# AdaLN block with four Mamba-2 layers and a mixture of experts: work of the mixer's steps moved between ScalarE and GpSimd, reordered, and four steps per loop body

## The chip, the cores and the metric

The kernel runs on one core of a Trainium2 chip. The metric is the device time of one launch in microseconds. Three runs of the kernel before took 1159.37, 1164.06 and 1163.69 us, median 1163.69 us.

## The reference

The input x has 8 batches of 512 tokens of width 128. With `sa, ca, ga, sb, cb, gb` six modulation vectors per batch:

```python
h = layernorm(x) * (1 + ca) + sa
for l in range(4):                                  # the mixer: four Mamba-2 layers
    n = rmsnorm(h) * block_norm_w[l]
    z, xBC, dt = split(n @ W_in[l])                 # 256, 512, 8 columns
    xBC = silu(causal_conv4(xBC))                   # four taps along the tokens
    xs, B, C = split(xBC)                           # 256, 128, 128
    dt = softplus(dt + dt_bias); dA = exp(-exp(A_log) * dt)
    hs = hs * dA + (dt * xs) B^T ; y = hs C         # a scan over 512 tokens, 8 heads of 32
    y = rmsnorm((y + D * xs) * silu(z)) * gate_norm_w
    h = h + y @ W_out[l]
x = x + ga * rmsnorm(h) * final_norm_w
x = x + gb * moe(layernorm(x) * (1 + cb) + sb)      # shared expert + top 2 of 8 experts
```

## The kernel before, in words

Tokens lie along the free dimension: a tile [128, 512] is one batch, its 128 partitions the model's width. `h` and `xT` hold all eight batches in SBUF. The scan over tokens is computed by chunks: each batch is cut into four chunks of 128 tokens. Within a chunk the result is a masked product of matrices; between chunks a state S of [128, 256] is carried (the recurrence: three states, S1 to S3).

The mixer has 32 steps, one per layer and batch; step k is layer k // 8, batch k % 8. Each engine runs its own list of instructions in order, and engines wait for one another by counting semaphores. The body of step k works on three batches at once: part A projects and convolves batch k, part B does the chunk products and the recurrence of batch j = k-1, part C the gated norm and output projection of batch i2 = k-2, and N prepares the norm of batch k+1. Steps 0 to 2 and 31 to 33 are written out; steps 3 to 30 are loops whose body holds two steps (`pairs_of_steps`, L227), 14 passes. SP and POOL have these 28 steps in three loops (`steps_with_weights`, L246): in steps 3 to 18 they also convert the experts' weights, 256 KB a step, for later (called weight steps here; the others are plain steps). After the mixer come the routing and the shared expert for each batch ("front") and 23 tiles of routed experts.

What a step holds, by engine, with the names used below:

- SP (L299): loads RW (weight steps), WO_raw after `wos_a` says that the one before was scaled, five of the six projection weights WA[t] after PE is done with each, then the small rows PC and P4, then WA[5].
- PE (L474): `dt` product (L487), `decays(0)` (L542, L548), G = B C^T (L573), `turn` of x and B (L527), `decays(1)`, `project(2)` (L494; a projection waits for the taps of the tile that used its bank: project(2) for tap(0,3), project(3) for tap(1,3)), `turn(3)`, `square_mean` (L503, L504; waits for ACT's sqy), `project(3)`, `project_out` (L510, L511), `decays(2)`, `within(0)` (L562; waits for DVE's scale_out, whose bank it overwrites), `project(4)`, `decays(3)`, `within(1)`, the mean of sqh (L619), `project(5)`, transposes (L632 to L634), `within(2)`, the states' products (L640, L641, L644), `within(3)`, two projections of the next step (L667), and `yi` (L658), which needs the states.
- ACT (L946): exponentials E0 to E7 (`decay_exp`, L951; En+2 waits for Mn, two buffers), softplus parts, `xtok` (L971), squares `sqy` (L1000), tap 0 of tiles 2, 3 and 1 (L963, L942), lnY and rY (L1018, L1020), `norm_square` (L850: copies WDT, the dt weights; L853: sqh = h squared), row_exp (L957), zraw (L1044), the scaling of WO (L1052, two of 128x128), `norm_log` and `norm_root` (L857, L862), and six SiLUs with a table load.
- DVE (L1341): conv taps of four tiles (tap(0,0) is L1350, the others L1354; tap(t, s) adds shift s of tile t and waits for the tap before it on that tile), causal (L1361), M0 to M7 (`apply_decay`, L1370), the scan of dA (L1379), `spend` (L1383), scale_out (L1389), `hn` (L1475), the recurrence (L1447, then twice `stmp` L1451 and S L1457), `yt` (L1465) and `ti` (L1470).
- POOL (L1619): dt_ (L1622), dtx and xw (L1630, L1635), the three-part split of cum (L1641 to L1648), wdec (L1650), weight conversion in weight steps (L1665, L1667), the update of h (L1671), own_rows (L1656), then for t = 0, 1 `yt` += `ti` (L1679) and y2 = yt * silu(z) (L1683), which wait for DVE's `ti`.

The order of taps and its neighbours on DVE (L1394):

```python
tap(0, 0); tap(0, 1); tap(0, 2); tap(1, 1); tap(0, 3); tap(1, 2)
causal_products(); apply_decay(0)
apply_decay(1)
tap(1, 3); running_sum()
```

Of the kernel before, what the change touches and what calls it, by code (L numbers as in the profile page):

```python
# [60 lines left out]
def build(nc, x, w_in, w_out, par, cst, c_t, wmod, par2, w1, w2, out):  # L61
    ctx = ExitStack()
    with ctx:
# [137 lines left out]
        wdt_a, hup, sqh_a, ms_mm, rb_a, hn_v = sem("wdt_a"), sem("hup"), sem("sqh_a"), sem("ms_mm"), sem("rb_a"), sem("hn_v")  # L201
# [5 lines left out]
        fin_v, fin_p, wos_a = sem("fin_v"), sem("fin_p"), sem("wos_a")  # L207
# [19 lines left out]
        def pairs_of_steps(eng, body, first, last, **kw):  # L227

            with eng.Fori(first // 2, last // 2) as i:
                for odd in (1, 0):  # L230
                    k = eng.snap(2 * i + (2 - odd))
                    body(k, odd, A=True, B=True, C=True, N=True, **kw)

        def steps(eng, body):


            body(0, 0, A=True, B=False, C=False, N=True)
            body(1, 1, A=True, B=True, C=False, N=True)
            body(2, 0, A=True, B=True, C=True, N=True)
            pairs_of_steps(eng, body, 3, STEPS - 1)  # L240
            body(STEPS - 1, 1, A=True, B=True, C=True, N=False)
            body(STEPS, 0, A=False, B=True, C=True, N=False)
            body(STEPS + 1, 1, A=False, B=False, C=True, N=False)

        def steps_with_weights(eng, body):
# [5 lines left out]
            pairs_of_steps(eng, body, 3, 3 + NE, W="up")  # L251
            pairs_of_steps(eng, body, 3 + NE, 3 + 2 * NE, W="down")
            pairs_of_steps(eng, body, 3 + 2 * NE, STEPS - 1)
# [23 lines left out]
        def _(sp):  # L277
# [26 lines left out]
            def body(k, odd, A, B, C, N, W=None):  # L304
# [6 lines left out]
                if B:  # L311
                    j = k - 1
                    at_j = sp.snap(j // NB * (2 * DM * P))

                    wait(sp, wos_a, 2 * j)
                    sp.dma_start(WO_raw[:, :], rows(w_out, at_j, 2 * DM)).then_inc(s_wo, 16)
# [89 lines left out]
        def _(pe):  # L406
# [30 lines left out]
            pe.wait_ge(sqh_a, 1)  # L437
# [37 lines left out]
            def body(k, odd, A, B, C, N):  # L475
# [5 lines left out]
                if A:  # L481

                    wait(pe, hn_v, k + 1)
                    wait(pe, wdt_a, k + 1)
# [21 lines left out]
                def project_out():  # L506
                    wait(pe, wos_a, 2 * (i2 + 1))
# [86 lines left out]
                if C and not B:  # L594
                    square_mean_of_h(1)
                if A:
                    project(3)
                if C:
                    project_out()
# [16 lines left out]
                if N:  # L616
                    wait(pe, sqh_a, k + 2)
# [199 lines left out]
        def _(act):  # L817
# [30 lines left out]
            def norm_square(n):  # L848
                wait(act, dt_mm, n)
                f(WDT[:, :], PAR[:, bass.ds(n // NB * NPAR + C_WDT, 32)], ACT.Copy).then_inc(wdt_a, 1)  # L850
                wait(act, hup, n + 1)
                wait(act, ms_mm, n)
                f(sqh[:, :], h[:, bass.ds(n % NB * L, L)], ACT.Square).then_inc(sqh_a, 1)  # L853

# [12 lines left out]
            norm_square(0)  # L867
# [77 lines left out]
            def body(k, odd, A, B, C, N):  # L945
# [83 lines left out]
                if N:  # L1029
                    norm_square(k + 1)  # L1030
                elif A:
# [13 lines left out]
                if B:  # L1045
                    row_exp(1)

                    wait(act, s_wo, 16 * (j + 1))
                    wait(act, out_mm, j)
                    gw = act.snap(j // NB * NPAR + C_GW)  # L1050
                    for t in range(2):
                        f(WO[:, t * DM:(t + 1) * DM], WO_raw[:, t * DM:(t + 1) * DM], ACT.Copy,  # L1052
                          scale=PAR[:, bass.ds(gw + t, 1)]).then_inc(wos_a, 1)
# [133 lines left out]
        def _(dve):  # L1187
# [149 lines left out]
            def body(k, odd, A, B, C, N):  # L1337
# [56 lines left out]
                if A:  # L1394
                    tap(0, 0)
                    tap(0, 1)
                    tap(0, 2)
                    tap(1, 1)
                    tap(0, 3)
                    tap(1, 2)  # L1400
                if B:
                    causal_products()
# [203 lines left out]
        def _(pool):  # L1606
# [9 lines left out]

            def body(k, odd, A, B, C, N, W=None):
# [54 lines left out]
                if A:  # L1672
                    own_rows(0)
                    own_rows(1)
                if B:

                    for t in range(2):
# [6 lines left out]

            steps_with_weights(pool, body)
# [121 lines left out]
```

## Time and profile before

| | |
|---|---|
| median of three runs | 1163.69 us |
| the profiled execution | 1162.99 us |
| its span, first to last instruction | 1161.0 us |
| mixer, steps 3 to 30 | about 99 to 751 us |
| busy, share of the span | PE 86%, DVE 84%, ACT 76%, POOL 58% |
| mean granted clock of TensorE | 0.952 |

The profile lists instructions by engine: PE is TensorE's matmul, PEld its weight load, DVE VectorE, ACT ScalarE, POOL GpSimd, SP the queue that issues DMAs. L1383 is line 1383 of the kernel. "Busy" leaves out waits, register and branch instructions. "Idle before" is the time that an engine stood before an instruction, and the name behind the arrow is what ended it; "issue" means that the profile shows nothing that it waited for. The chain that ended last follows the work back from the last instruction to what released each.

### The profile page before, as it was taken

To read this page: it belongs to the slowest core of one execution; us is meant where nothing else is said; L and a number is where in the kernel's file an instruction comes from. 1 tells how busy PE (TensorE), PEld (TensorE's weight loads), DVE (VectorE), ACT (ScalarE), POOL (GpSimd) and SP (SyncE) were. 2 spreads that over 40 slices of the span, in tenths; PEclk is the share of its full clock that TensorE was granted. 3 is DMA by queue.
4 is the path that set the end of the run, shared out by engine and by line. 5 is a ranking of instruction groups with operands and counts; after the bars stand their busy time and mean duration, and the time that the engine had idled before them with its cause. 6 is when DMAs were issued, how large, how long until landed. Compare 5 with 4: busy or idle time off the path is not lost.

```text
span 1161.0 us, 25184 instructions
## 1 busy us (share of the span) xinstructions
PE 993.7 (86%) x6136; PEld 559.7 (48%) x6136; DVE 977.1 (84%) x1801; ACT 884.2 (76%) x1724; POOL 676.3 (58%) x853
## 2 busy tenths in 40 slices
PE   5799999999899999999999999985788767999980
PEld 4244544445444444454445444542444445777760
DVE  6779999999999999999999998974778775888865
ACT  5688999999899999999999999984556534655640
POOL 0267577766776677656655765672244551666661
PEclk9789999999999999999999999998888888999995
DMA  5111242224222432210001000100000115676638
GB/s 141 34 34 33 89 156 86 88 87 153 91 86 87 142 102 86 78 32 22 22 23 31 22 22 23 27 7 1 19 28 28 37 33 180 223 232 226 223 116 217
DMA packets 85584, 97.84 MB, mean 84 GB/s; under 512 B 20698, under 2 KB 65888, under 8 KB 85536
## 3 DMA queue, kind: packets, MB, share of 16 engines
q1 hardware_dynamic: 80544, 88.83, 24.2%
q0 software_dynamic: 4992, 8.48, 2.2%
q8 instruction: 18, 0.29, 0.1%
q14 instruction: 30, 0.25, 0.1%
HBM read 59.67 MB, written 37.83 MB: 84 GB/s over the span
## 4 chain that ended last, share of the span: by engine, by line
PE 35%; DVE 26%; issue 18%; ACT 6%; POOL 3%; DVEq 2%; DMA 1%; ACTq 0%; SPq 0%; POOLq 0%
DVE cv L1354 9%; PE bank L494 4%; PE bank L562 4%; PE bank L681 2%; PE bank L667 2%; DVE M L1370 2%; PE bank L683 2%; PE bank L682 2%; DVE cv L1350 2%; PE bank L619 2%; PE bank L693 2%; PE bank L695 2%; PE bank L692 2%; PE bank L658 2%; PE bank L640 2%
## 5 line engine op out<-in xcount | busy, mean ns | idle before, releaser
L1354 DVE SCALAR_TENSOR_TENSOR cv<-bank,PAR,cv 128x511 f32<-128x511 f32 (+2 forms) x384 | 274.1, 742 | 15.7 <-ACT cv L963 2.8
L1370 DVE SCALAR_TENSOR_TENSOR M<-E,bank 128x512 f32<-128x512 f32 x256 | 168.3, 678 | 20.7 <-ACT E L951 11.4
L1679 POOL TENSOR_TENSOR yt<-yt,ti 128x384 f32<-128x384 f32 x64 | 64.0, 1000 | 203.6 <-DVE ti L1470 203.6
L494 PE MATMUL bank<-hn,WA 128*128 128x512 f32 x256 | 144.9, 649 | 41.0 <-DVE cv L1354 40.6
L951 ACT ACTIVATE E<-bank 128x512 f32<-128x512 f32 x256 | 149.0, 595 | 31.9 <-DVE M L1370 30.1
L1710 POOL DMA_INDIRECT RS<-y,XR x92 | 98.8, 1074 | 78.7 <-DVE y L1567 55.4
L1703 POOL DMA_INDIRECT XS<-stage,IDX x64 | 65.9, 1029 | 79.2 <-DVE run L1329 62.1
L1101 ACT ACTIVATE hr<-bank,W1B 128x512 f32<-128x512 f32 x92 | 63.4, 689 | 56.7 <-PE bank L683 49.8
L562 PE MATMUL bank<-M,dtx 128*32 128x128 f32 x2048 | 82.9, 279 | 15.6 <-DVE o_sb L1389 15.1
L494 PEld LDWEIGHTS bank<-hn,WA 128*128 128x128 f32 x256 | 40.6, 194 | 111.9 <-issue 74.0
L1497 DVE TENSOR_TENSOR hL<-hr,hH 128x512 fp32r<-128x512 f32 x124 | 87.1, 702 | 4.3
L1683 POOL TENSOR_TENSOR y<-yt,zs 128x512 f32<-128x512 f32 x64 | 81.6, 1274 | 9.8 <-POOL yt L1679 7.0
L1656 POOL TENSOR_TENSOR own<-p,selb 128x512 bf16<-128x512 bf16 x64 | 72.7, 1157 | 15.5 <-PE bank L548 15.5
L1630 POOL TENSOR_TENSOR dtx<-xtok,DTW 128x256 f32<-128x256 f32 x128 | 80.6, 630 | 1.0 <-ACT xtok L971 1.0
L562 PEld LDWEIGHTS bank<-M,dtx 128*32 128x32 f32 x2048 | 49.2, 109 | 59.5 <-issue 53.2
L1495 DVE CAST hH<-hr 128x512 fp32r<-128x512 f32 x124 | 54.3, 438 | 25.6 <-ACT hr L1101 12.1
L1082 ACT ACTIVATE xbc<-cv 128x512 f32<-128x512 f32 x128 | 72.9, 619 | 0.0
L667 PE MATMUL bank<-hn,WA 128*128 128x512 f32 x128 | 65.2, 632 | 1.4 <-ACT zs L1086 0.8
L542 PE MATMUL bank<-nselb,PC 32*128 32x512 bf16 x256 | 61.3, 388 | 0.3 <-ACT E L951 0.2
L1635 POOL TENSOR_TENSOR xw<-xtok,DTW 128x256 f32<-128x256 f32 x96 | 60.9, 634 | 0.0
L971 ACT ACTIVATE xtok<-bank 128x384 f32<-128x384 f32 x128 | 56.2, 508 | 2.5 <-PE bank L527 2.4
L658 PEld LDWEIGHTS bank<-xbc,S 128*128 128x128 f32 x384 | 47.6, 191 | 17.8 <-DVE S L1457 13.6
(245 smaller groups left out, 2633.8 us busy)
## 6 DMA issues: line engine op xcount, KB each, us to landing
XS<-PADT SPq DMA_DIRECT2D x32, 520.0 KB, 4.3
WA<-w_in SPq DMA_DIRECT2D x192, 64.0 KB, 1.8
W1B<-WD SPq DMA_DIRECT2D x23, 514.0 KB
W2B<-WD SPq DMA_DIRECT2D x23, 512.5 KB
WD<-WS SPq DMA_DIRECT2D x16, 512.0 KB, 2.7
XR<-XS SPq DMA_DIRECT2D x23, 260.0 KB
RW<-w_in SPq DMA_DIRECT2D x18, 256.0 KB, 4.4
WO_raw<-w_out SPq DMA_DIRECT2D x32, 128.0 KB, 3.6
```

The costliest lines, as they stand in the source:

```text
L494: mm(bank[t % 2][:, :], WA[t][:, :], hn[:, :], start=True, stop=True).then_inc(pj_mm, 1)
L562: ins = mm(bank[6 + hh // 4][q:q + 32, c * CH:(c + 1) * CH], dtx[c][:, hh * HD:(hh + 1) * HD], M[2 * (hh // 4) + c % 2][:, (hh % 4) * CH:( ...
L667: mm(bank[t][:, :], WA[t][:, :], hn[:, :], start=True, stop=True).then_inc(pj_mm, 1)
L951: f(E[i % 2][:, :], bank[2 + i % 2][:, :], ACT.Exp).then_inc(e_a, 1)
L1082: f(conv_rows(t, odd), cv[t][:, :], ACT.Silu).then_inc(silu_a, 1)
L1354: stt(out=cv[t][:, s:L], in0=src[:, 0:L - s], scalar=PAR[:, bass.ds(cw + 3 - s, 1)], in1=cv[t][:, s:L], op0=ALU.mult, op1=ALU.add).then_in ...
L1370: stt(out=M[i % 4][:, :].rearrange("p (n t) -> p n t", n=4), in0=E[i % 2][:, :].rearrange("p (n t) -> p n t", n=4), scalar=1.0, in1=bank[5 ...
L1497: tt(hL[t][:, :], hr[t][:, :], hH[t][:, :].bitcast(F32), ALU.subtract).then_inc(hl_v, 1)
L1630: tt(dtx[c][:, :].rearrange("p (h d) -> p h d", h=NH), xv, DTW[:, 32 * c:32 * c + NH].unsqueeze(2).to_broadcast([P, NH, HD]), ALU.mult).th ...
L1656: tt(own[:, g * 512:(g + 1) * 512].rearrange("p (h t) -> p h t", h=4), p2[:, :].unsqueeze(1).to_broadcast([P, 4, CH]), selb[:, g * 512:(g ...
L1683: tt(y2[t][:, :], yt[t][:, :], zs[:, bass.ds((j % 2) * 2 * L + t * L, L)], ALU.mult).then_inc(fin_p, 1)
L1710: nc.gpsimd.indirect_dma_start(RS[:, :], bass.IndirectOffsetOnAxis(ap=XR[i % XD][:, (c + 1) * ROW - 1:(c + 1) * ROW].bitcast(I32), axis=0) ...
```

## The change

The mixer's steps are changed in five places. On DVE the three shifts of tile 0 follow one another, and tap(1, 2) comes behind the causal product. On PE `project_out` comes ahead of `project(3)`. The square of h for the norm is made by POOL, for the batch after the next, and in most steps waits until DVE has made the second `stmp` of the recurrence (`s_v`, 5j+4); ACT makes only the first one. POOL also copies WDT and scales WO, behind own_rows. The loops have four steps per body: 7 passes on PE, ACT and DVE; 2, 2 and 3 on SP and POOL. In `steps` and `steps_with_weights` every call of `pairs_of_steps` becomes one of `fours_of_steps`; the semaphores are renamed with their engine.

```diff
-        def pairs_of_steps(eng, body, first, last, **kw):
-            with eng.Fori(first // 2, last // 2) as i:
-                for odd in (1, 0):
-                    k = eng.snap(2 * i + (2 - odd))
-                    body(k, odd, A=True, B=True, C=True, N=True, **kw)
+        def fours_of_steps(eng, body, first, last, **kw):
+            with eng.Fori(first // 4, last // 4) as i:
+                for n in range(4):
+                    k = eng.snap(4 * i + (3 + n))
+                    body(k, (3 + n) % 2, A=True, B=True, C=True, N=True, **kw)
...
@@ sync: body, if B @@
-                    wait(sp, wos_a, 2 * j)
+                    wait(sp, wos_p, 2 * j)
                     sp.dma_start(WO_raw[:, :], rows(w_out, at_j, 2 * DM)).then_inc(s_wo, 16)
...
@@ tensor: body @@
                 if C and not B:
                     square_mean_of_h(1)
-                if A:
-                    project(3)
                 if C:
                     project_out()
+                if A:
+                    project(3)
...
@@ scalar @@
-            def norm_square(n):
-                wait(act, dt_mm, n)
-                f(WDT[:, :], PAR[:, bass.ds(n // NB * NPAR + C_WDT, 32)], ACT.Copy).then_inc(wdt_a, 1)
-                wait(act, hup, n + 1)
-                wait(act, ms_mm, n)
-                f(sqh[:, :], h[:, bass.ds(n % NB * L, L)], ACT.Square).then_inc(sqh_a, 1)
...
-            norm_square(0)
+            f(WDT[:, :], PAR[:, C_WDT:C_WDT + 32], ACT.Copy).then_inc(wdt_done, 1)
+            act.wait_ge(hup, 1)
+            f(sqh[:, :], h[:, 0:L], ACT.Square).then_inc(sqh_done, 1)
...
-                if N:
-                    norm_square(k + 1)
-                elif A:
+                if A and not N:
                     square_h(0)
...
-                    wait(act, s_wo, 16 * (j + 1))
-                    wait(act, out_mm, j)
-                    gw = act.snap(j // NB * NPAR + C_GW)
-                    for t in range(2):
-                        f(WO[:, t * DM:(t + 1) * DM], WO_raw[:, t * DM:(t + 1) * DM], ACT.Copy,
-                          scale=PAR[:, bass.ds(gw + t, 1)]).then_inc(wos_a, 1)
                     decay_exp(6)
...
@@ vector: body @@
                     tap(0, 2)
+                    tap(0, 3)
                     tap(1, 1)
-                    tap(0, 3)
+                if B:
+                    causal_products()
+                if A:
                     tap(1, 2)
                 if B:
-                    causal_products()
                     apply_decay(0)
...
@@ gpsimd @@
+            def square_h(n):
+                hb = h[:, bass.ds(n % NB * L, L)]
+                wait(pool, hup, n + 1)
+                wait(pool, ms_mm, n)
+                tt(sqh[:, :], hb, hb, ALU.mult).then_inc(sqh_done, 1)
+
+            def step_weights(n):
+                wait(pool, dt_mm, n)
+                tt(WDT[:, :], PAR[:, bass.ds(pool.snap(n // NB * NPAR + C_WDT), 32)], ones_row[:, 0:32], ALU.mult).then_inc(wdt_done, 1)
+
+            def output_weights(n):
+                gw = pool.snap(n // NB * NPAR + C_GW)
+                wait(pool, s_wo, 16 * (n + 1))
+                wait(pool, out_mm, n)
+                for t in range(2):
+                    tt(WO[:, t * DM:(t + 1) * DM], WO_raw[:, t * DM:(t + 1) * DM], PAR[:, bass.ds(gw + t, 1)].to_broadcast([P, DM]),
+                       ALU.mult).then_inc(wos_p, 1)
...
                     own_rows(0)
                     own_rows(1)
-                if B:
+                if N:
+                    step_weights(k + 1)
+                if B:
+                    output_weights(j)
+                if N and not B:
+                    square_h(k + 2)
+                if B:
+                    if N:
+                        wait(pool, s_v, 5 * j + 4)
+                        square_h(k + 2)
                     for t in range(2):
                         wait(pool, fin_v, 4 * j + 3 + t)
...
+            pool.wait_ge(const_v, 3)
+            square_h(1)
             steps_with_weights(pool, body)
```

## Rows read from the trace of the kernel before

**Rows 1.** Busy us (instructions) of each engine, granted clock, DMA share, GB/s, by stretch
```profile
286.00:477.00 191.00, 176.07 (x1259) 91.34 (x1258) 176.33 (x286) 175.22 (x361) 137.34 (x179) 1.00 0.32 108
477.00:751.00 274.00, 254.29 (x1806) 130.19 (x1804) 250.78 (x416) 252.38 (x523) 172.59 (x238) 1.00 0.09 25
```

**Rows 2.** The chain that ended last, 543 to 569 us: start, us, what
```profile
555.38 0.65 PE bank L562 x16
...
567.42 0.82 DVE cv L1350
```

**Rows 3.** Timeline of DVE, plain steps: start, us, what, [idle before <-releaser]
```profile
560.55 0.69 DVE L1370 SCALAR_TENSOR_TENSOR M<-E,bank 128x512 f32<-128x512 f32 x1 [0.52 <-ACT E L951]
...
563.58 0.42 DVE L1451 TENSOR_TENSOR stmp<-S,dec 128x256 f32<-128x256 f32 x1
...
577.13 0.74 DVE L1354 SCALAR_TENSOR_TENSOR cv<-bank,PAR,cv 128x510 f32<-128x510 f32 x1
577.96 0.69 DVE L1389 TENSOR_TENSOR o_sb<-bank,rY 128x512 f32<-128x512 f32 x1
...
590.36 0.80 DVE L1350 TENSOR_SCALAR cv<-bank,PAR 128x512 f32<-128x512 f32 x1
```

**Rows 4.** Timeline of ACT, one plain step
```profile
550.19 0.60 ACT L951 ACTIVATE E<-bank 128x512 f32<-128x512 f32 x1 [0.65 <-DVE M L1370]
...
553.76 0.21 ACT L850 ACTIVATE WDT<-PAR 128x32 f32 x1
...
554.40 0.76 ACT L963 ACTIVATE cv<-bank,PAR 128x512 f32<-128x512 f32 x1
...
557.17 0.60 ACT L1044 ACTIVATE zraw<-bank 128x512 f32<-128x512 f32 x1 [0.66 <-PE bank L494]
```

**Rows 5.** Timeline of PE, the same step
```profile
548.00 1.12 PE L494 MATMUL bank<-hn,WA 128*128 128x512 f32 x2 [0.61 <-DVE cv L1354]
```

**Rows 6.** Timeline of POOL, the same step
```profile
557.87 2.27 POOL L1656 TENSOR_TENSOR own<-p,selb 128x512 bf16<-128x512 bf16 x2 [1.12 <-PE bank L548]
566.43 0.99 POOL L1679 TENSOR_TENSOR yt<-yt,ti 128x384 f32<-128x384 f32 x1 [6.29 <-DVE ti L1470]
```

**Rows 7.** What line L1350, tap(0,0) on DVE, sat idle for: us, times
```profile
  issue: 5.3, 13
```

**Rows 8.** Timeline of DVE, two weight steps
```profile
188.04 0.75 DVE L1475 SCALAR_TENSOR_TENSOR hn<-h,PAR,rB 128x512 f32<-128x512 f32 x1 [0.26 <-issue]
...
207.38 0.97 DVE L1383 TENSOR_SCALAR spend<-CST,p 128x32 bf16<-128x32 f32 x1
```

**Rows 9.** Timeline of POOL, the same two weight steps
```profile
185.56 2.28 POOL L1656 TENSOR_TENSOR own<-p,selb 128x512 bf16<-128x512 bf16 x2
...
207.03 1.28 POOL L1671 TENSOR_TENSOR h<-h,o_sb 128x512 f32 x1
```

**Rows 10.** Line L1383: duration min/median/max in ns, first and last start
```profile
L1383 DVE TENSOR_SCALAR spend<-CST,p x32: 230/494/1144, 41.4 to 764.9; 128x32 bf16<-128x32 f32 x32
```

**Rows 11.** Line L1379, the scan, likewise
```profile
L1379 DVE TENSOR_TENSOR_SCAN cum<-ones_row,dA x32: 417/703/878, 37.0 to 759.1; 128x128 f32<-128x128 f32 x32
```

**Rows 12.** Groups of ACT, 60 to 830 us: count, busy us, mean ns
```profile
L1052 ACT ACTIVATE WO<-WO_raw,PAR 128x128 f32<-128x128 f32 x64 | 22.1, 400 | 0.0
```

**Rows 13.** Groups of POOL, likewise
```profile
L1650 POOL TENSOR_TENSOR wdec<-dt_,ecs 128x128 f32<-128x128 f32 x31 | 14.1, 455 | 0.0
```

**Rows 14.** Timeline of DVE at the start
```profile
26.20 2.23 DVE L1228 TENSOR_SCALAR sqy<-xin,mv,rstd 128x128 f32 x8 [0.30 <-issue]
```

**Rows 15.** Part 3 of the page: packets, MB, share, of the instruction queues
```profile
q8 instruction: 18, 0.29, 0.1%
q14 instruction: 30, 0.25, 0.1%
```

**Rows 16.** Part 6 of the page: DMA issues, KB each, us to landing
```profile
WA<-w_in SPq DMA_DIRECT2D x192, 64.0 KB, 1.8
...
RW<-w_in SPq DMA_DIRECT2D x18, 256.0 KB, 4.4
```

More of the change, by code:

```diff
@@ L200, in build @@
         s_wo, p4_in = sem("wo_in"), sem("p4_in")
-        wdt_a, hup, sqh_a, ms_mm, rb_a, hn_v = sem("wdt_a"), sem("hup"), sem("sqh_a"), sem("ms_mm"), sem("rb_a"), sem("hn_v")
+        wdt_done, hup, sqh_done, ms_mm, rb_a, hn_v = sem("wdt_done"), sem("hup"), sem("sqh_done"), sem("ms_mm"), sem("rb_a"), sem("hn_v")
         dt_mm, pj_mm, silu_a, dtc_v, dta_a, tr_mm = sem("dt_mm"), sem("pj_mm"), sem("silu_a"), sem("dtc_v"), sem("dta_a"), sem("tr_mm")
@@ L206, in build @@
         px_p, st_mm, s_v, e2_mm, e2_a, yi_mm = sem("px_p"), sem("st_mm"), sem("s_v"), sem("e2_mm"), sem("e2_a"), sem("yi_mm")
-        fin_v, fin_p, wos_a = sem("fin_v"), sem("fin_p"), sem("wos_a")
+        fin_v, fin_p, wos_p = sem("fin_v"), sem("fin_p"), sem("wos_p")
         sq_a, ss_mm, ry_a, out_mm, o_v = sem("sq_a"), sem("ss_mm"), sem("ry_a"), sem("out_mm"), sem("o_v")
@@ L239, in steps @@
             body(2, 0, A=True, B=True, C=True, N=True)
-            pairs_of_steps(eng, body, 3, STEPS - 1)
+            fours_of_steps(eng, body, 3, STEPS - 1)
             body(STEPS - 1, 1, A=True, B=True, C=True, N=False)
@@ L250, in steps_with_weights @@
             body(2, 0, A=True, B=True, C=True, N=True, W="shared")
-            pairs_of_steps(eng, body, 3, 3 + NE, W="up")
-            pairs_of_steps(eng, body, 3 + NE, 3 + 2 * NE, W="down")
-            pairs_of_steps(eng, body, 3 + 2 * NE, STEPS - 1)
+            fours_of_steps(eng, body, 3, 3 + NE, W="up")
+            fours_of_steps(eng, body, 3 + NE, 3 + 2 * NE, W="down")
+            fours_of_steps(eng, body, 3 + 2 * NE, STEPS - 1)
             body(STEPS - 1, 1, A=True, B=True, C=True, N=False)
@@ L436, in _ @@
             pe.wait_ge(const_v, 2)
-            pe.wait_ge(sqh_a, 1)
+            pe.wait_ge(sqh_done, 1)
             mm(bank[0][:, :], mean128[:, :], sqh[:, :], start=True, stop=True).then_inc(ms_mm, 1)
@@ L483, in body @@
                     wait(pe, hn_v, k + 1)
-                    wait(pe, wdt_a, k + 1)
+                    wait(pe, wdt_done, k + 1)
                     wait(pe, s_v, 5 * j - 2)
@@ L506, in project_out @@
                 def project_out():
-                    wait(pe, wos_a, 2 * (i2 + 1))
+                    wait(pe, wos_p, 2 * (i2 + 1))
                     if B:
@@ L595, in body @@
                     square_mean_of_h(1)
+                if C:
+                    project_out()
                 if A:
                     project(3)
-                if C:
-                    project_out()
                 if C and not B:
@@ L616, in body @@
                 if N:
-                    wait(pe, sqh_a, k + 2)
+                    wait(pe, sqh_done, k + 2)
                     wait(pe, zc_a, k + 1)
```

## The prediction

> **What bounds the kernel now.** I read the views in this order: busy time by stretch, the chain of waits, the timelines of ACT, PE, DVE and POOL over two plain steps and two weight steps, then single lines. The mixer's 32 steps take some 750 of 1161 us, and in its plain steps (from 477 us on, where no expert weights are converted) PE, DVE and ACT are each busy over 91% of the time, at clock 1.00 [rows 1]. So no share decides; the chain does. It runs from DVE's scale_out to PE's `within(0)` at 555.38, then along PE without a gap (decays, `within`, projections, states, `yi`) to some 566.4, then through DVE's `ti` and the return of DVE's loop to the next tap(0,0) at 567.42 [rows 2], and along DVE to the next scale_out at 577.96 [rows 3]. The cycle is thus DVE for 10.5 us, PE for 11, and `ti`. ACT has slack: it stands 0.65 us before E2 for DVE's M0 and 0.66 us before zraw for PE [rows 4]; PE stands 0.61 us for a tap [rows 5]. Once a step DVE waits for ACT, 0.52 us ahead of the eighth M [rows 3], of which 0.25 to 0.3 are more than issue; behind it the recurrence meets PE's state products, which come no earlier. POOL stands 6.29 us before `yt`, for `ti` [rows 6].
>
> A step without a return of the loop at its end lasts 590.36-567.42 = 22.94 us [rows 2, 3]. The return costs DVE 0.41 us of idle "issue" (5.3 us over 13 returns [rows 7]) and the 0.08 us by which two independent DVE instructions overlap: 0.48. In the 16 steps that convert expert weights a second thing happens. `spend` (L1383, 128x32) takes 0.23 us where nothing meets it, 0.49 in the median, and 0.97 behind each return [rows 8, 10]. There it runs from 207.38 to 208.35, and POOL's h update from 207.03 to 208.31 [rows 9]: it ends when POOL's instruction ends. In the step that has no return ahead of it DVE is 0.48 us earlier against POOL and meets the end of the instruction before (0.50).
>
> **Four steps per body.** 28 steps in 7 passes in place of 14: 13 taken returns become 6. 7 x 0.48 = -3.4 us. And of the 8 weight steps that begin behind a return 4 are left: 4 x (0.97-0.50) = -1.9 us. This is DVE's; PE, ACT and POOL return behind queued work or a wait. Bounds: from nothing (PE sets the step instead) to -5.3.
>
> **Taps in a row.** DVE starts an independent instruction 0.66 us after a tap and a dependent one 0.23 later. tap(0,3) directly behind tap(0,2): +0.23. tap(1,2) between causal and M0 removes the dependent start of M0: -0.27. Net -0.04 a step, -1.1 us over 28. tap(0,3) itself ends 0.44 us earlier, so project(2), for which PE stood 0.61 us [rows 5], starts earlier. That gains nothing alone: square_mean behind it waits for ACT's sqy, and `within(0)`, the next thing that PE owes the cycle, waits for scale_out in any case.
>
> **Output projection ahead of project(3).** project(3) waits for tap(1,3) and leaves PE a hole of some 0.4 us, which the four passes of the output projection now cover. project(3) then ends near where the output projection ended before. What comes earlier is scale_out: in a step behind a return it starts 0.83 us after tap(2,2) (577.96-577.13 [rows 3]), where 0.66 would do. That is 0.17 us; in weight steps `spend` swallows it, since POOL's instruction ends when it ends. 3 x 0.17 = -0.5 us. Bounds 0 and 28 x 0.17 = -4.8.
>
> **Squares and scalings on POOL.** ACT loses L850 and L853, 554.40-553.76 = 0.64 us [rows 4], and two scalings of 0.40, 0.3 from start to start [rows 12]: 1.2 us a step, all of it out of slack. What is late next is E7, which waits for M5 and shares ACT with lnm: 0.1 to 0.2 us earlier, inside DVE's wait ahead of M7; then `S` waits for PE's states instead. I take 0; bounds 0 and 28 x 0.3 = -8.4 (the wait ahead of M7 goes and PE follows).
> POOL gains the square (1.28 us, as the h update [rows 9]), two 128x128 products and one 128x32 (0.46 or less [rows 13]), 2.6 us. The square waits for the second `stmp`, which ends at 564.00 [rows 3], so it would run from 564.1 to 565.4; `yt` starts at 566.43 [rows 6]. Hidden, with 1 us to spare. Queued behind it is that `yt`, for which sqy and square_mean wait, and these have 1 us until scale_out; if the cover went the square would first cost 0.3 us a step. PE asks for sqh a step later. SP's load of WO_raw waits for a scaling that is now some 3 us later, still before SP reaches it; the WA loads queued behind it wait for PE as before.
> The small products have less room. In weight steps own_rows ends at 185.56+2.28 = 187.84 [rows 9] and `hn` starts at 188.04 [rows 8]: the three run from 187.9 to 189.1, beside `hn` and the first `stmp`, which both read two SBUF tensors. The scan, also such, takes 0.42 us alone, 0.70 in the median and 0.88 at most, beside POOL [rows 11]. So 0 to 0.5 us per such step; DVE's tail has 0.2 us free before ti[1] waits for PE. I take 0.1 for the 12 weight steps without a return ahead: +1.2; bounds 0 and +6. In plain steps own ends at 560.14 [rows 6], well ahead of `hn`: 0.
> POOL's square beside `yt` and the last state sum, which read one tensor from PSUM, is in no row. If they met as `spend` does, up to 28 x 0.5 = +14; I take 0, as the taps (one PSUM input) keep 0.74 us beside POOL. The Trainium skill (GPSIMD Engine Reference, Key points) has POOL contend only with DVE instructions in a two-port mode or with two SBUF inputs, which agrees with `spend` and the scan and would leave `yt` free.
>
> **Start.** The first square for step 1 runs on POOL from about 25 to 26.3 us, amid DVE's L1228 (SBUF to SBUF), whose last eight end at 28.4 just before hn [rows 14]. Blocked as `spend` is: up to +1.27; I take +0.6. In step 0 project(2) comes 0.4 us earlier: -0.4.
>
> **Sum.** -3.4 -1.9 -1.1 -0.5 +1.2 +0.6 -0.4 = -5.5. The profiled execution took 1162.99 us (span 1161.0), so 1157.5. The median of the three runs, 1163.69, is 0.7 above that execution.
>
> **Rivals.**
> A, slower: an engine no longer holds the longer body, and each return fetches instructions. DVE has 35 working instructions a step (x416 in some 12 steps [rows 1]), so 70 a body before and 140 now, waits and register work on top. Against it: 70, and PE's 300, return without a fetch now, since 18 and 30 instruction packets, 0.54 MB, are all that the run read [rows 15]. For it: no row shows that twice as much is held. A stall has no row either; the nearest are loads from issue to landing, 1.8 us for 64 KB and 4.4 for 256 KB [rows 16]. On DVE all of it lies in the cycle: 6 x 1.8 to 4.4 = 11 to 26; at 2.5 us +15: 1172.5. From 0.9 us per return on it outweighs the gain. On ACT alone, the 1.3 us of slack and the 1.2 set free take most of it: 1158 to 1162.
> The Trainium skill (Runtime: NRT & Kernel Launch, Instruction fetch mechanics) states this: 32 KiB of instructions for most engines, 128 for PE, filled in sequence, and a taken branch to a block not held stalls for a fetch. It gives blocks of 16 KiB; the second kind of packet here is 8 KB.
> B, no gain: the small products hold `hn` and `stmp` by 0.5 us, and POOL's new timing makes `spend` 0.97 in all 16 weight steps: +4.8 and +5.7 on the forecast, 1168 at worst, 1163 with half of each.
> C, faster: the wait ahead of M7 was worth its 0.3 us: another -8.4, 1149.
> D: returns cost nothing, as PE sets the step in the end: 1162.8.
>
> **Chances.** Forecast 0.42, A on DVE 0.26, A on ACT alone 0.07, B 0.10, C 0.10, D 0.05. The forecast's own range is 1153 to 1161. 0.5% below the median is 1157.9 (about what a measurement can tell from no change); 0.30 of the 0.42 lies under it. Faster 0.30 + 0.10 = 0.40; slower A 0.25 + B 0.02 = 0.27; same 0.33. Range: low 1150 (most of C), high 1176 (A up to 3 us per return).
>
> **What would show it.** Starts of tap(0,0) 22.9 us apart three times in a body and 23.3 once; DVE idle ahead of L1350 for 0.4 us 6 times. With A it is 2 us or more, and instruction packets come all through the mixer. `spend` 0.97 us in 4 weight steps, 0.5 in 12. POOL's square from the second `stmp` to before `ti`. ACT idle for 1.2 us more a step with the steps unchanged. `hn` and `stmp` near 0.75 and 0.42 us. I am wrong if plain steps average over 23.15 or under 22.7 us.

## The result, and the profile after

| | before | after |
|---|---|---|
| median of six runs each | 1161.53 us | 1174.96 us |
| lowest and highest | 1157.09, 1164.06 | 1170.37, 1179.20 |
| the profiled execution, and its span | 1162.99, 1161.0 us | 1174.94, 1173.1 us |
| the 28 loop steps, first tap(0,0) of step 3 to that of step 31 | 652.24 us | 669.70 us |
| busy PE, DVE, ACT, POOL | 86, 84, 76, 58% | 86, 83, 73, 64% |

The change made the kernel slower: the ratio is 1.0114, 95% interval 1.0077 to 1.0151. The forecast was 1157.5 us; rival A had the direction and gave 1172.5 us.

The chain of waits of the kernel after, 183 to 206 us, across a return (start, us, what; DVEq is DVE's sequencer, L229 the line of the loop):

```profile
186.61 0.52 DVE ti L1458
187.16 0.07 DVEq L229
187.23 4.18 issue
191.41 0.09 DVEq L229
...
191.97 0.82 DVE cv L1336
...
195.53 2.08 PE bank L494 x2
197.60 0.64 PE bank L527 x3
198.24 1.71 PE bank L503 x2
```

What tap(0,0), now L1336, and the first table load of an ACT step, L968, sat idle for (two answers, one after the other), which answer to [rows 7]:

```profile
  issue: 24.5, 6
...
  issue: 17.4, 6
```

DVE stands 4.1 us on average at each of its 6 returns, where it stood 0.41 us at each of 13. ACT, which stood for nothing there, stands 2.9 us on average. DVE's six stalls are not equal: 4.34, 4.91, 4.83 and 4.44 us where the return ends a weight step, 2.93 and 3.06 us in plain steps. One of each kind, and then the stretches in which DVE stands there (columns as in [rows 1], the last two DMA share and GB/s):

```profile
388.90 0.81 DVE L1336 TENSOR_SCALAR cv<-bank,PAR 128x512 f32<-128x512 f32 x1 [4.83 <-issue]
...
579.71 0.81 DVE L1336 TENSOR_SCALAR cv<-bank,PAR 128x512 f32<-128x512 f32 x1 [2.93 <-issue]
```

```profile
383.70:388.90 5.20, 2.12 (x20) 1.24 (x12) 0.37 (x2) 1.95 (x4) 4.45 (x4) 0.98 0.73 235
...
576.80:579.70 2.90, 1.72 (x12) 1.15 (x11) 0.00 (x0) 1.25 (x1) 2.66 (x3) 1.00 0.03 10
```

The instruction queues over the whole run, against 18 and 30 packets before [rows 15], and then their packets between 100 and 760 us, in the kernel after:

```profile
q14 instruction: 99, 0.81, 0.2%
q8 instruction: 21, 0.34, 0.1%
...
q14 instruction: 73, 0.60, 0.3%
q8 instruction: 6, 0.10, 0.1%
```

A second loss stands behind the stall. The timeline of the kernel after around the same return, 187 to 196.5 us:

```profile
189.47 1.28 ACT L968 ACT_TABLE_LOAD   x1 [2.53 <-issue]
191.03 0.36 ACT L975 ACTIVATE u<-bank,PAR 128x128 f32<-128x128 f32 x1
191.44 2.18 PE L527 MATMUL bank<-CST,xbc 128*128 128x128 f32 x9 [2.07 <-ACT u L975]
191.97 0.81 DVE L1336 TENSOR_SCALAR cv<-bank,PAR 128x512 f32<-128x512 f32 x1 [4.34 <-issue]
```

And busy time by stretch, columns as in [rows 1]: eight of the us behind that return, the whole step and the two after it, then the plain steps:

```profile
192.00:200.00 8.00, 7.55 (x20) 3.75 (x19) 7.55 (x12) 5.51 (x14) 4.85 (x10) 0.50 0.04 11
...
191.97:216.70 24.73, 23.92 (x141) 11.67 (x139) 21.11 (x35) 18.76 (x37) 14.96 (x24) 0.82 0.16 57
216.70:239.71 23.01, 21.46 (x154) 11.18 (x153) 21.74 (x36) 20.40 (x41) 19.48 (x27) 1.00 0.33 113
239.71:262.50 22.79, 21.50 (x154) 11.16 (x153) 21.46 (x37) 20.28 (x41) 19.31 (x27) 1.00 0.28 94
...
477.00:751.00 274.00, 254.48 (x1751) 133.26 (x1744) 240.94 (x406) 235.65 (x465) 192.64 (x276) 0.97 0.11 31
```

PE stands 2.07 us for ACT's `u`, and its granted clock falls: between 192 and 200 us it is 0.50, that is 1.2 GHz instead of 2.4, and the two records of project(2) take 2.08 us where project(3) of full clock takes 1.03. All six steps behind a return have a mean clock of 0.81 to 0.93; before, every loop step had 1.00. In the plain steps one pass of four lasts, from tap(0,0) to tap(0,0), 23.8, 22.4, 22.7 and 25.8 us. The two undisturbed steps are shorter than any before (22.94, 23.36); the stall in the last and the clock in the first take back nearly three times as much (3.3 us for 1.2 in a pass).

**How executions are compared here.** A single profile differs from the next by up to 5.4 us before the loops begin: in some executions PE's clock is 0.53 between 54 and 60 us (the profile of before is one) and step 1 lasts 27.4 us, in others, as that of after, it is 1.00 and step 1 lasts 22.0; some lie between (23.5, 24.5, 26.1). It comes and goes between kernels whose start is the same, line for line. This stretch in before, and in before with four steps per body (columns as in [rows 1]):

```profile
54.00:60.00 6.00, 6.00 (x19) 2.95 (x17) 3.72 (x7) 3.74 (x10) 4.32 (x8) 0.53 0.04 11
```

```profile
54.00:60.00 6.00, 5.13 (x29) 2.37 (x33) 5.89 (x10) 6.00 (x18) 4.15 (x8) 1.00 0.04 11
```

So below the 28 loop steps are compared, where kernels that should agree do so within 0.3 us (650.87 and 650.63, 632.57 and 632.60 below), and beside them the ratio of the timed runs.

### The profile page after: what moved, and what is told of

Same layout as the page of the kernel before. It is cut to its first block, busy times and chain, and to the rows that moved or that the text cites. A ratio compares the mean times of both kernels' runs of the same rounds, so it can differ in the third digit from the quotient of the medians.

```text
span 1173.1 us, 25001 instructions
## 1 busy us (share of the span) xinstructions
PE 1006.5 (86%) x6136; PEld 570.3 (49%) x6136; DVE 970.7 (83%) x1801; ACT 853.1 (73%) x1598; POOL 748.6 (64%) x980
## 4 chain that ended last, share of the span: by engine, by line
PE 43%; DVE 22%; issue 16%; ACT 8%; POOL 4%; DMA 3%; DVEq 2%; SPq 1%; ACTq 1%; POOLq 0%
DVE cv L1340 9%; PE bank L494 6%; PE bank L562 4%; PE bank L681 3%; PE bank L667 3%; DVE M L1356 2%; PE bank L683 2%; PE bank L682 2%; PE bank L619 2%; PE bank L658 2%; PE bank L693 2%; PE bank L695 2%; PE bank L692 2%; DVE cv L1336 2%; DMA XS<-stage,IDX 1%
## 5 line engine op out<-in xcount | busy, mean ns | idle before, releaser
L1340 DVE SCALAR_TENSOR_TENSOR cv<-bank,PAR,cv 128x511 f32<-128x511 f32 (+2 forms) x384 | 280.3, 742 | 20.3 <-ACT cv L958 3.2
L1356 DVE SCALAR_TENSOR_TENSOR M<-E,bank 128x512 f32<-128x512 f32 x256 | 167.8, 676 | 13.7 <-ACT E L946 11.6
L1610 POOL TENSOR_TENSOR sqh<-h 128x512 f32 (+1 forms) x32 | 33.3, 1042 | 105.2 <-DVE stmp L1439 80.6
L1697 POOL TENSOR_TENSOR yt<-yt,ti 128x384 f32<-128x384 f32 x64 | 64.0, 999 | 51.1 <-DVE ti L1458 51.1
L494 PEld LDWEIGHTS bank<-hn,WA 128*128 128x128 f32 x256 | 43.4, 196 | 77.9 <-issue 54.4
L1483 DVE CAST hH<-hr 128x512 fp32r<-128x512 f32 x124 | 54.3, 438 | 24.5 <-ACT hr L1087 21.0
L527 PE MATMUL bank<-CST,xbc 128*128 128x128 f32 x384 | 59.5, 297 | 16.4 <-ACT u L975 16.4
L527 PEld LDWEIGHTS bank<-CST,xbc 128*128 128x128 f32 x384 | 50.1, 154 | 37.4 <-ACT u L975 17.8
```

The costliest lines, as they stand in the source:

```text
L494: mm(bank[t % 2][:, :], WA[t][:, :], hn[:, :], start=True, stop=True).then_inc(pj_mm, 1)
L527: ins = nc.tensor.transpose(bank[TURN_BANK[c]][:, n * P:(n + 1) * P], conv_rows(t, odd + 1, c * CH, CH), ident)
L1340: stt(out=cv[t][:, s:L], in0=src[:, 0:L - s], scalar=PAR[:, bass.ds(cw + 3 - s, 1)], in1=cv[t][:, s:L], op0=ALU.mult, op1=ALU.add).then_in ...
L1356: stt(out=M[i % 4][:, :].rearrange("p (n t) -> p n t", n=4), in0=E[i % 2][:, :].rearrange("p (n t) -> p n t", n=4), scalar=1.0, in1=bank[5 ...
```

## The experiments

"After" and "before" name the kernels that an experiment starts from. All but the last were timed in three rounds, or five where it is said, each against runs of before on the same chip; the last (e16_three_no_stall) is a single execution. First the loops.

**Two steps per body in the kernel after** (label e1_pairs): all five engines.

```diff
-            fours_of_steps(eng, body, 3, STEPS - 1)
+            pairs_of_steps(eng, body, 3, STEPS - 1)
```

> The changed kernel with two steps per loop body again on every engine; all its other edits stay. Theory (the longer body is not held, and each of 6 returns stalls DVE for 4.3 us and ACT for 2.5): the stalls go, DVE's idle before tap(0,0) falls from 24.5 us over 6 times to about 5.3 over 13, the instruction packets of the second kind fall from 99 to about 30, and the time to 1145 us (1140 to 1150), since the steps without a return already last 22.4 to 23.0 us. Rival (the other edits cost time too, by POOL holding hn, and the loop is only part of it): 1160 us or more.

Measured: 1156.57 us, ratio 0.9972 (0.9953 to 0.9990); 28 steps 650.87 us, idle "issue" again 5.3 us over 13 returns. The sign came out, the size did not: what is left of the change gains 1.4 us in the loops, and the time lies 11.6 us above the 1145 expected. The whole loss lies in the number of steps per body.

**Four steps per body in the kernel before** (e3_fours_only):

```diff
-            pairs_of_steps(eng, body, 3, STEPS - 1)
+            fours_of_steps(eng, body, 3, STEPS - 1)
```

> The kernel before with four steps per body and nothing else changed. Theory: six stalls with what they delay, some 30 us, less 3.4 us for the returns saved: 1185 us (1178 to 1193). Rival (the stall comes from the other edits, or hits less where ACT has more to do): 1160 to 1175 us.

Measured: 1183.72 us, ratio 1.0203 (1.0171 to 1.0235); 28 steps 674.49 us. As expected: +22.25 us by this edit alone.

**No loops** (e2_written_out from after, e10_before_written_out from before):

```diff
+        def written_out(eng, body, first, last, **kw):
+            for k in range(first, last):
+                body(k, k % 2, A=True, B=True, C=True, N=True, **kw)
```

> The changed kernel with the 28 steps written out on every engine, no loop at all. Theory (only a return to instructions no longer held stalls; a run straight on is fetched ahead): no idle of 4 us anywhere, the 13 short returns of the pairs go as well, 1139 us (1134 to 1145), with 100 or more instruction packets. Rival (it is the amount of fetched instructions that costs): 1165 us or more, idle spread over all steps.

> The kernel before with all its 28 loop steps written out, no loops in the mixer. The changed kernel written out took 1140.2, with steps of 22.59 us set by PE. Theory: what the loops cost (return, register instructions ahead of each addressed instruction) is nearly all of the difference between 1156 and 1140, and the other edits add little: 1140 to 1146, steps of 22.6 to 22.8 us. Rival: the other edits only pay where no return is in the way, and without them ACT and DVE set the step at 22.9: 1148 to 1152.

Measured: from after 1140.21 us, ratio 0.9835 (0.9799 to 0.9871), 28 steps 630.88 us; from before 1137.80 us, ratio 0.9818 (0.9799 to 0.9838), 28 steps 632.57 us. Both beat both kernels. In neither trace does an engine stand over 0.9 us for "issue" in these steps. Without loops the timed runs tell nothing of what the other edits are worth; the 28 steps are 1.7 us shorter with them, in one profile each.

**Which engine stalls.** Four steps per body as after, with two on the engines named: DVE alone (e4_dve_pairs), ACT alone (e5_act_pairs), both (e6_dve_act_pairs).

```diff
-            steps(dve, body)
+            steps(dve, body, pairs_of_steps)
```

> The changed kernel with two steps per body on DVE alone, four on PE, ACT, POOL and SP. Theory (each engine that loops over more than it holds stalls by itself): DVE's 4.3 us go, ACT's 2.5 us stay and now set the step behind a return, so half to two thirds of the loss is recovered: 1155 us (1149 to 1162). Rival (ACT's stall lies in its slack): 1145 to 1149 us, as with pairs everywhere.

> The kernel after, with two steps per body on ACT alone and four on DVE, PE, SP and POOL. With DVE's four and ACT's two the other way round (the run before this) the time was 1179. Theory: both engines lie in the step's chain, so either stall alone costs what both together cost, since they fall at the same place of the step and overlap: DVE idle 'issue' some 4 us ahead of 6 tap(0,0), ACT's 0, time 1172 to 1180. Rival: ACT's stall was the one that cost, and DVE's 4 us is hidden behind PE: 1157 to 1162.

> The kernel after, with two steps per body on DVE and ACT, and four on PE, SP and POOL. Theory: PE, SP and POOL lose nothing by the longer body (POOL returns behind a wait, PE holds its longer body or fetches ahead): 1154 to 1158, as with two steps everywhere (1156.6), instruction packets fewer than 60. Rival 1: POOL's longer body is fetched at each return, 2 to 4 us, and moves its dt_ and the three-part split that PE's decays need: 1162 to 1170. Rival 2: PE stalls: over 1170.

| two steps per body on | us | ratio | 28 steps | who stalls |
|---|---|---|---|---|
| none (after) | 1174.96 | 1.0114 | 669.70 | DVE 24.5 us, ACT 17.4 us |
| DVE | 1179.09 | 1.0159 (1.0113 to 1.0205) | 673.06 | ACT 19.7 us |
| ACT | 1179.00 | 1.0169 (1.0147 to 1.0192) | 672.73 | DVE 24.2 us |
| DVE and ACT | 1157.63 | 0.9987 (0.9967 to 1.0007) | 650.63 | none |

The first of these missed: with DVE held, ACT's stall alone costs as much as both. The second and third came as expected; PE, POOL and SP lose nothing that shows by four steps (650.63 us against 650.87). Who waited for whom with DVE held, 384 to 396 us, across a return of ACT (us in all, times, longest):

```profile
ACT L980 <- issue: 4.4, 1, 4.4
...
PE bank L539 <- ACT u L987: 4.0, 1, 4.0
POOL dt_ L1643 <- ACT ln L997: 2.9, 1, 2.9
DVE cum L1377 <- ACT dA L1012: 1.7, 1, 1.7
```

The stall lies ahead of `u`, and PE's turns of x and B cannot write the bank before `u` has read it. ACT's slack lies later in the step, ahead of E2 and zraw, and is no help.

**DVE alone written out, from before** (e11_dve_written_out):

> The kernel before, with its 28 loop steps written out on DVE alone; SP, PE, ACT and POOL keep loops of two. All written out took 1137.8, the 28 steps from tap(0,0) of step 3 to that of step 31 took 632.6 us against 652.2 in loops. Theory: nearly all of these 20 us were DVE's (its return, the later start of instructions whose address is in a register, and POOL's instructions met by spend and hn because of it): 28 steps in 632 to 638 us, time 1139 to 1146. Rival: each engine's loop has its share, PE's above all, since PE sets the step of 22.6 us that is left: 28 steps in 642 to 650 us, time 1148 to 1158.

Measured: 1141.50 us, ratio 0.9834 (0.9809 to 0.9860); 28 steps 632.60 us, all that writing out everything gives. DVE's timeline there, one plain step:

```profile
525.75 0.80 DVE L1362 TENSOR_SCALAR cv<-bank,PAR 128x512 f32<-128x512 f32 x1
526.59 3.50 DVE L1366 SCALAR_TENSOR_TENSOR cv<-bank,PAR,cv 128x511 f32<-128x511 f32 x5
530.00 0.69 DVE L1373 TENSOR_TENSOR bank<-bank,causal 128x512 f32<-128x512 f32 x1
530.79 1.28 DVE L1382 SCALAR_TENSOR_TENSOR M<-E,bank 128x512 f32<-128x512 f32 x2
...
541.74 0.69 DVE L1382 SCALAR_TENSOR_TENSOR M<-E,bank 128x512 f32<-128x512 f32 x1 [0.61 <-ACT E L963]
542.34 0.75 DVE L1487 SCALAR_TENSOR_TENSOR hn<-h,PAR,rB 128x512 f32<-128x512 f32 x1
543.40 0.43 DVE L1459 COPY S<-bank 128x256 f32<-128x256 f32 x1 [0.31 <-PE bank L653]
```

The same places in the loop of before, 544 to 568 us:

```profile
544.04 0.80 DVE L1350 TENSOR_SCALAR cv<-bank,PAR 128x512 f32<-128x512 f32 x1
544.99 3.61 DVE L1354 SCALAR_TENSOR_TENSOR cv<-bank,PAR,cv 128x511 f32<-128x511 f32 x5
548.52 0.69 DVE L1361 TENSOR_TENSOR bank<-bank,causal 128x512 f32<-128x512 f32 x1
549.41 1.28 DVE L1370 SCALAR_TENSOR_TENSOR M<-E,bank 128x512 f32<-128x512 f32 x2 [0.20 <-DVE bank L1361]
...
561.50 0.75 DVE L1475 SCALAR_TENSOR_TENSOR hn<-h,PAR,rB 128x512 f32<-128x512 f32 x1 [0.26 <-issue]
```

From the eighth M to `hn` it is 561.50-560.55 = 0.95 us in the loop and 0.60 written out; from tap(0,0) to the next tap 0.95 and 0.84; from the causal product to M0 0.89 and 0.79. With half a return (0.24) that makes 0.35+0.11+0.10+0.24 = 0.80 us a step, and the plain steps fell from a mean of 23.15 to 22.38. The starts are measured; that register instructions of the loop fill them is the reading that fits, since writing out changes nothing else on DVE but the return. In the step shown PE is what DVE then meets: the copy of S waits 0.31 us for its state product.

**Fourteen steps per body on PE, ACT and DVE, from after** (e12_fourteens), one return instead of six:

```diff
+            with eng.Fori(first // 14, last // 14) as i:
+                for n in range(14):
+                    k = eng.snap(14 * i + (3 + n))
```

> The kernel after, with 14 steps per body on PE, ACT and DVE (one return instead of six) and two on SP and POOL. Theory: what is paid is the return, not the length of the body, since the engine reads ahead as long as it runs straight on: one stall of about 4 us ahead of tap(0,0) of step 17, all other steps as the undisturbed ones of the kernel after (22.8 to 23.0 us in weight steps, 22.4 to 22.7 in plain ones): 28 steps in 638 to 645 us against 669.7, time 1142 to 1150. Rival: a long body is read slowly throughout, or several times in a pass, and steps away from the return also lose: over 655 us, 1160 or more.

Measured: 1151.24 us, ratio 0.9918 (0.9890 to 0.9945); 28 steps 643.14 us. What tap(0,0) sat idle for:

```profile
  issue: 5.1, 1
```

The 28 steps came as expected, the time just above its range (1142 to 1150): one stall, one step of 27.96 us, 23.34 behind it, all others between 22.4 and 23.0. PE, whose body has fourteen steps here too, stands 3.42 us for "issue" at its one return, where no such idle shows with four. The price hangs on the return: DVE's stall of 5.1 us behind fourteen steps is near the 4.3 to 4.9 behind four, in a weight step as well.

**The other edits alone**, each in before with two steps per body, five rounds: the order of taps (e7_taps_only), the output projection (e8_project_only), squares and scalings on POOL (e9_pool_only); their diffs are the hunks of the change.

> The kernel before (two steps per body), with only the new order on DVE: tap(0,3) behind tap(0,2), tap(1,2) behind the causal product. The prediction gave it -0.04 us a step, -1.1 in all: ratio 0.999. Rival: it gives the whole -3.2 us of the kernel after with two steps per body (plain steps 22.78 and 23.33 us there, 22.94 and 23.36 before), as project(2) no longer makes PE stand: ratio 0.997. Or it costs, as M0 and M1 come later for the product within(0): above 1.001.

> The kernel before (two steps per body), with only the output projection ahead of project(3). The prediction gave it -0.5 us in all (bounds 0 and -4.8): ratio 0.9995. Rival: scale_out starts 0.17 us earlier in every step: ratio 0.996. Rival: project(3) later moves conv tile 3 on ACT and costs: above 1.001.

> The kernel before (two steps per body), with only the squares and the scalings moved from ACT to POOL. The prediction gave it +1.2 beside hn and the second stmp, +0.6 at the start, 0 elsewhere: ratio 1.0015. In weight steps hn is 0.92 us against 0.75 in every second step. Rival: ACT's relief ends the wait ahead of the eighth M: -0.3 us a step, ratio 0.993 to 0.997. Rival: POOL's contention costs 0.5 us in each of the 16 weight steps: ratio 1.007.

| | us | ratio | 28 steps less those of before (weight, plain steps) | prediction, for two per body |
|---|---|---|---|---|
| taps | 1161.00 | 1.0006 (0.9988 to 1.0024) | -1.05 (+0.33, -1.38) | -1.1 |
| output projection | 1157.63 | 0.9982 (0.9967 to 0.9998) | -1.03 (+0.19, -1.22) | -1.0 (6 x 0.17) |
| squares, scalings | 1160.31 | 1.0003 (0.9988 to 1.0018) | +0.14 (+0.38, -0.24) | +0.8 (8 x 0.1) |

The timed ratios of the first and third tell nothing at this size; the steps do, in one profile each, and +0.14 is within the 0.3 us by which such profiles differ. In plain steps the taps give 22.94 to 22.85 and 23.36 to 23.21 us, in weight steps nothing. The output projection gives the 0.17 us in each plain step that begins behind a return (22.94 to 22.77), where it was forecast. The sum, -1.9, stands against -1.4 for all three together.

**Stall or clock.** Extra matmuls of 128x384 on PE, whose result is not used, at the start of the first step of each body: seven in after (e13_filled), seven where nothing stalls (e14_filled_no_stall, from e6_dve_act_pairs), three in after (e15_filled_three), three where nothing stalls (e16_three_no_stall).

```diff
+                    if fill:
+                        for _ in range(7):
+                            mm(bank[4][:, 0:384], mean128[:, :], hn[:, 0:384], start=True, stop=True)
```

> The kernel after (four steps per body), with seven extra matmuls of 128x384 on PE at the start of the first step of each body; their result is not used. In the kernel after, PE stands 1.6 to 3.8 us in that step for the stalled ACT, and the granted clock of the step falls to between 0.81 and 0.93, at half speed for some 8 us. Theory: a good part of a return's price is this clock, not the stall; kept busy, PE keeps more of its clock, in which case the 28 steps take 655 to 664 us against 669.7 and the granted clock of these steps is over 0.95: time 1160 to 1169. Rival: the stall alone is the price, and the clock costs nothing because DVE sets the step: 669 to 676 us, the extra matmuls adding what they cost: 1174 to 1182.

> The control of the run with seven extra matmuls: the same matmuls in the kernel with two steps per body on DVE and ACT and four on PE, SP and POOL, where nothing stalls (28 steps 650.6 us, 1157.6). It tells what the matmuls cost by themselves: seven times 2.3 us of PE at the start of a step, 0 if DVE's taps cover them, 16 us if they lie in the chain. Expected: 2 to 8 us, 28 steps 653 to 659 us, time 1159 to 1166.

> The kernel after with three extra matmuls in place of seven. Seven took 4.5 us of PE (two passes of 0.32 us each), not the 2.3 I had counted; the granted clock stayed at 1.00 in every step, the steps that follow a return lost 0.2 to 1.7 us, and the return steps stayed as they were. Their control cost 2.5 us per body, so PE has some 2 us to spare there, and three matmuls (1.9 us) should cost nothing. If they are enough to hold the clock: return steps at most 27.3 and 25.3 us (the stall alone on top of 22.8 and 22.4), next steps 22.7 to 23.4, 28 steps 655 to 663 us, time 1160 to 1168. If they are not: clock 0.81 to 0.93 in these steps as without them, 28 steps 668 to 671 us, time 1173 to 1177. Rival: the clock holds and the return steps keep their 27.3 to 28.2 and 25.7 us, as the stall alone sets them: 28 steps 663 to 666 us.

> Control of the run with three extra matmuls: the same three in the kernel with two steps per body on DVE and ACT and four on PE, SP and POOL, where nothing stalls. Expected: nothing or up to 0.3 us per body, 28 steps 650.6 to 653 us.

| | us | 28 steps | clock of the six steps behind returns |
|---|---|---|---|
| seven, in after | 1177.07 | 669.15 | 1.00, all |
| seven, no stall | 1179.82 | 669.85 | 1.00, all |
| three, in after | 1177.85 | 667.05 | 0.93, 1.00, 0.86, 0.86, 1.00, 1.00 |
| three, no stall | 1166.20 (one execution) | 652.35 | 1.00, all |

Seven took twice the PE time that I had counted and cost 19 us where nothing stalls, for the 2 to 8 expected, so their time in after decides nothing, though it lies where the rival of that run had it. The steps do, and three hold the clock at three of six returns, which sets one kernel's steps side by side. The step that ends in the return to step 23 and the step behind it, in after and then with three extra matmuls:

```profile
554.01:579.71 25.70, 23.27 (x165) 12.26 (x164) 20.92 (x37) 21.21 (x41) 19.20 (x27) 1.00 0.08 24
579.71:603.52 23.81, 22.77 (x142) 11.75 (x142) 20.84 (x35) 19.87 (x41) 14.08 (x23) 0.86 0.09 25
```

```profile
559.38:585.10 25.72, 24.48 (x170) 12.92 (x170) 20.91 (x36) 21.08 (x41) 19.21 (x27) 1.00 0.09 24
585.10:607.71 22.61, 20.14 (x146) 10.26 (x144) 20.66 (x35) 19.69 (x41) 14.00 (x23) 1.00 0.09 26
```

The step with the stall is the same to 0.02 us; the step behind it loses 1.2 us by the clock. At the return to step 11, a weight step, the stalled step is 27.79 us with the clock held and 27.84 without, the next one 23.31 and 25.02. With seven matmuls, clock 1.00 in all six, the six steps behind returns last 139.1 us together and 144.1 in after: the clock's part is 5.1 us of the some 26 that six stalled returns cost more than held ones. It is at least that, since the matmuls' own cost lies in the 139.1: behind the two plain returns three of them give back 1.2 and 1.1 us, seven 0.6 and 0.5. That the stall alone sets the stalled step is what the rival in the expectation for three matmuls had; its 663 to 666 us for the 28 steps were missed by 1.05, with three clocks of six held instead of all. Against after they fell by 2.65 us, in one profile each; the timed runs (1174.04 to 1185.45) show no gain. Three matmuls cost 1.7 us where nothing stalls, and three of six clocks are about half of 5.

## Why the prediction was wrong

- **Four steps per body: this step failed.** It priced a return as 0.48 us of DVE, plus what `spend` meets behind it, and took 7 of 13 away. What was shown is the opposite case, rival A. With the returns alone changed the 28 steps grew by 22.25 us (forecast -5.3). The saving itself was real: in the run with fourteen steps per body, its stalled step and the next set to their neighbours' length, the 28 steps come to some 637.6 us, so by this estimate the 13 returns of two per body cost (650.9-637.6)/13 = 1.0 us each, and seven fewer are worth -7. Each of the six that are left then costs (669.7-650.9+7)/6 = 4.3 us more than a return that is held. Against the undisturbed steps beside it the stalled step is longer by 3.0 and 3.1 us in plain steps and 4.5 to 5.1 in weight steps, each time DVE's stall there and 0.05 to 0.17 us more; some 0.85 us of clock come in the step behind. Rival A's price was 2.5 us, from loads that land in 1.8 to 4.4 [rows 16]; that range held the mean, its middle did not, and three of the six stalls lie above it. The plain steps average 23.36 us in after, over the 23.15 that the prediction named as a sign of being wrong.
- **The chance of that rival, 0.26, could be read from no row.** [rows 15] show that a body of two is held and say nothing of four. What weighs the packets came only with the runs: written out, DVE's 26 further steps add 10 packets to q14's 30, 3.1 KB a step; in the run with fourteen per body ACT and DVE read 42 more than with two, over 52 steps, 6.6 KB a step, since values computed from the loop's register bring instructions of their own. By that estimate a body of two is 13 KB and one of four 26 KB. A return that stalls DVE or ACT alone brings some 5 packets: q14 reads 68 and 67 packets in these two runs and 36 where neither stalls, 32 and 31 more over six returns. That is some 40 KB, more than the body. The Trainium skill (Runtime: NRT & Kernel Launch, Instruction fetch mechanics) says that most engines hold two blocks of 16 KiB, filled in sequence, and that a branch to a block not held waits for it; a body of 26 KB, not aligned to blocks, lies in up to three. These runs agree on the stall, on straight code being free of it, and on PE holding more (no stall with four steps, 3.42 us with fourteen); no run here shows the block.
- **ACT alone: wrong.** The prediction let 1.3 us of slack and the 1.2 set free take most of an ACT stall: 1158 to 1162. It was 1179. The slack was read rightly and lies at the wrong place: ahead of E2 and zraw, while the return is ahead of `u`, for which PE waits. Where two engines of the cycle stall at one time, the cost is that of one.
- **Taps in a row: the sum right, partly by luck**, -1.05 us against -1.1. The working gave -0.04 us in each of 28 steps; measured were -0.07 to -0.17 in each plain step and +0.33 in all in the 16 weight steps, and why was not tested.
- **Output projection: right**, -1.03 us where its own working gives -1.0 for two per body; the -0.5 of the sum was for four.
- **Squares and scalings: mechanism right, its price in the step too large.** POOL's square runs where forecast, behind the second `stmp`, and takes less, 1.04 us and not 1.28; beside it the two `yt` of DVE take 1.40 us, as before, so the 0 taken for them was right; `yt` stands 51.1 us for `ti` over 32 steps, 1.6 each, so it stays hidden. ACT works 31 us less (853.1 against 884.2) and nothing follows. The small products do meet `hn`: alone, these edits bring it from 0.75 to 0.90 us in 8 weight steps (mean of all 751 to 791 ns), 1.2 us of DVE, and in after it takes 0.91 to 1.03 us in 13 of the 16 weight steps, none of them behind a return. `stmp` stays at 0.42. The steps move by +0.14 us in all, +0.38 in weight steps, for +0.8 forecast, so most of the 1.2 is covered. DVE's group of `hn` before, and in the run with these edits alone:

```profile
L1475 DVE SCALAR_TENSOR_TENSOR hn<-h,PAR,rB 128x512 f32<-128x512 f32 x32 | 24.0, 751 | 9.9 <-issue 7.3 <-PE bank L494 2.6
```

```profile
L1473 DVE SCALAR_TENSOR_TENSOR hn<-h,PAR,rB 128x512 f32<-128x512 f32 x32 | 25.3, 791 | 11.4 <-issue 7.3 <-PE bank L506 4.2
```

- **Start: about right for the square, nothing for step 0.** tap(0,0) of step 0 starts at 32.4 us on average in the eight executions with POOL's square up to fourteen per body, at 31.9 in the six without: +0.5 for +0.6, though the two groups overlap (32.0 to 32.7 and 31.5 to 32.5). Step 0 itself lasts 19.2 us on average in both, with 18.3 to 20.2 in the second group; the -0.4 does not show.
- **`spend`: the count right, the reason wrong.** Forecast were 0.97 us in the 4 weight steps that begin behind a return and 0.50 in 12. In after it takes 1.09 us in 4 and 0.49 to 0.51 in 12, but the 4 are steps 4, 8, 12 and 16, the second of each pass; behind the stalled returns to steps 7, 11 and 15 it takes 0.50. That the count held is luck. Steps 7 and 8:

```profile
206.69 0.50 DVE L1369 TENSOR_SCALAR spend<-CST,p 128x32 bf16<-128x32 f32 x1
229.49 1.09 DVE L1369 TENSOR_SCALAR spend<-CST,p 128x32 bf16<-128x32 f32 x1
```

- **Rivals B and C** (POOL's new work costs it all; the wait ahead of M7 was worth 8.4 us) are excluded by two steps per body with all other edits: the 28 steps fall by 1.4 us.
- **Rival D** (PE sets the step in the end, returns cost nothing) is excluded: without DVE's loop the steps fall to 22.75 and 22.38 us.

Still open: why DVE's stall is 4.3 to 4.9 us in weight steps and 2.9 to 3.1 in plain ones, which is what makes the stalled steps differ. While DVE stands, the DMA share is 0.62 to 0.88 at the weight returns and 0.02 and 0.03 at the plain ones; that the loads of weights delay the fetch fits this, and no run separates the two. Nor was the longest body that is held looked for: two steps are, four are not.

## What to carry to other kernels

A longer loop body does not only mean fewer returns: beyond what an engine holds, each return is a stall on that engine (here 2.9 to 5.1 us on DVE), and it is enough that one engine of the cycle is over. Before unrolling by two, compare the count of instruction packets with the number of passes, and write the loop out altogether on the one engine that sets the step; here DVE alone gave all 20 us of the 28 steps. When an engine stalls, ask where in its order the stall lands, not how much slack it has in a step, and look at the granted clock of the steps behind.

## What the runs showed of the hardware that was not expected

- A stall on ACT that lets PE stand for 1.6 to 3.8 us is followed by PE at 1.2 GHz at every one of the six returns of after, for 3.4 to 10 us; where DVE alone stalls and PE stands for a tap instead, the six steps have a mean clock of 0.86 to 0.93. Three extra matmuls (2.1 us of PE at the start of the step) avoided it at three returns of six, seven at all.
- A loop costs far more than its return. Of the 0.77 us that a plain step lost when DVE was written out, 0.24 are the return; nearly all of the rest lies ahead of dependent instructions whose address, or the value that they wait for, is computed from the loop's register.
- A matmul of 128x384 in f32 shows two records, 0.33 us apart, so seven cost 4.5 us, and not the 2.3 that I took.
- With the same instructions at the start, PE's clock between 54 and 60 us is either 1.00 or 0.53 to 0.72, which moves an execution by up to 5.4 us. The spread of the runs (1157 to 1164 us before) is of that size; that it comes from there was not shown.
